# First attention layer: one full-width block of value matmuls between the two pairs of the next key tile; the rows of ones written at the end of the former batch

## The reference

```python
tokens = x.reshape(B, C, N).transpose(0, 2, 1)
qkv = (tokens @ w_proj + b_proj).reshape(B, N, NUM_HEADS, 3 * HEAD_DIM)
q, k, v = jnp.split(qkv, 3, axis=-1)
attn = jnp.einsum('bihd,bjhd->bijh', q, k) * SCALE
attn = jax.nn.softmax(attn, axis=2)
res = jnp.einsum('bijh,bjhd->bihd', attn, v).reshape(B, N, NUM_HEADS * HEAD_DIM)
out = res @ w_out + b_out + tokens
```

## Time and profile before

| | us |
|---|---|
| median of 3 runs | 3213.33 |
| lowest, highest | 3209.35, 3216.2 |
| span of the profiled execution, first to last instruction | 3214.9 |
| TensorE busy / VectorE / ScalarE / GpSimd | 2731.7 / 2212.3 / 1234.2 / 657.1 |
| matmuls | 16502 |
| mean granted TensorE clock (1 is 2.4 GHz) | 0.924 |

### The profile page before, as it was taken

The page is one execution under the profiler, slowest core; times in us unless marked ns, Lnnn a source line. Parts: engine busy times, 40 slices in busy tenths (PEclk is TensorE's granted clock), DMA queues, the critical chain, the costliest instruction groups (busy, mean ns, idle before and its releaser), DMA issues.

```text
span 3214.9 us, 45307 instructions
## 1 busy us (share of the span) xinstructions
PE 2731.7 (85%) x16502; PEld 1884.4 (59%) x16502; DVE 2212.3 (69%) x2474; ACT 1234.2 (38%) x1348; POOL 657.1 (20%) x397
## 2 busy tenths in 40 slices
PE   5889969899798897988879888798887998878983
PEld 4447754577545774457744677447764477644772
DVE  4766668666686675866668666785677756777666
ACT  2443325433254332543335333353333533244333
POOL 0430115201061021500225002340024300243011
PEclk8989989999899998999989999899988999889996
DMA  6100050000500004000040000400022000310015
GB/s 152 23 24 1 1 120 6 24 1 14 113 1 24 1 14 113 1 24 1 14 112 1 24 1 32 95 1 24 1 64 62 24 1 1 92 35 24 1 53 235
DMA packets 46400, 124.77 MB, mean 39 GB/s; under 512 B 9792, under 2 KB 21312, under 8 KB 42560
## 3 DMA queue, kind: packets, MB, share of 16 engines
q1 hardware_dynamic: 46144, 121.41, 14.1%
HBM read 43.01 MB, written 23.86 MB: 21 GB/s over the span
## 4 chain that ended last, share of the span: by engine, by line
PE 65%; DVE 12%; issue 9%; SPq 4%; DMA 4%; ACT 4%; DVEq 0%; ACTq 0%
PE tile L1264 22%; PE pv L1264 10%; PE tile L1358 8%; PE pv L1374 6%; PE tile L1336 5%; DVE small L871 4%; PE tile L1518 4%; SPq L445 4%; PE tile L1395 3%; DMA stack<-ones 2%; PE tile L1540 2%; PE tile L1648 1%; PE tile L1567 1%; PE tile L1417 1%; DMA stack<-qk_r 1%
## 5 line engine op out<-in xcount | busy, mean ns | idle before, releaser
L871 DVE TENSOR_REDUCE small<-tile 128x1 f32<-128x1024 f32 x512 | 610.6, 1219 | 210.9 <-PE tile L1336 210.1
L660 ACT ACTIVATE p<-tile 128x1024 f32<-128x1024 f32 x512 | 520.9, 1023 | 568.9 <-PE tile L1358 564.5
L1358 PE MATMUL tile<-stack 112*128 112x512 f32 x1024 | 387.0, 462 | 129.5 <-DMA stack<-ones 87.8
L547 POOL TENSOR_TENSOR acc<-acc,p 128x1024 f32<-128x1024 f32 x160 | 397.6, 2505 | 176.9 <-DVE acc L903 175.0
L1264 PE MATMUL tile<-qk_r 128*128 128x512 f32 x1536 | 378.0, 395 | 0.0
L1336 PE MATMUL tile<-stack 96*128 96x512 f32 x1024 | 339.8, 424 | 34.9 <-DMA stack<-qk_r 31.0
L1358 PEld LDWEIGHTS tile<-stack 112*128 112x128 f32 x1024 | 162.9, 196 | 350.7 <-issue 227.5
L572 POOL TENSOR_TENSOR row_sum<-act 128x256 f32<-128x256 f32 x32 | 42.1, 1335 | 1488.9 <-DVE act L1099 1488.9
L1374 PE MATMUL pv<-p,v 128*32 128x256 f32 (+1 forms) x3584 | 321.2, 431 | 9.4 <-ACT p L660 7.6
L1264 PEld LDWEIGHTS tile<-qk_r 128*128 128x128 f32 x1536 | 287.1, 188 | 66.6 <-issue 7.7
L1104 DVE TENSOR_TENSOR pl<-p,ph 128x1024 fp32r<-128x1024 f32 x128 | 158.2, 1236 | 238.2 <-ACT p L745 238.2
(11 more groups left out here) (277 smaller groups left out, 4356.9 us busy)
## 6 DMA issues: line engine op xcount, KB each, us to landing
stack<-qk_r SPq DMA_DIRECT2D x192, 256.0 KB, 5.0
x_in<-in_x_dram SPq DMA_DIRECT2D x9, 1024.0 KB, 7.6
act<-in_x_dram SPq DMA_DIRECT2D x8, 1024.0 KB, 11.0
x_scratch<-act SPq DMA_DIRECT2D x7, 1024.0 KB, 3.9
z_scratch<-zbuf SPq DMA_DIRECT2D x7, 1024.0 KB, 5.1
stack<-ones SPq DMA_DIRECT2D x8, 512.0 KB, 10.1
w3f<-w3f_scratch SPq DMA_DIRECT2D x8, 512.0 KB, 3.3
fin_rest<-z_scratch SPq DMA_DIRECT2D x3, 1024.0 KB, 12.6
```

The source lines that it names most:

```text
L547: pe.tensor_tensor(total, first, p0[:, jt % DEPTH, pair, :], ALU.add).then_inc(pool_done, gps.one("add0", *u, jt, pair))
L660: sc.activation(p0[:, jt % DEPTH, pair, :], tile_wait(b, "st0", *u, jt, pair), ACT.Exp, scale=float(D) ** -0.5).then_inc(scalar_done, scal ...
L871: ve.tensor_reduce(maxima[:, h * NT + it:h * NT + it + 1], t[:], X, ALU.max).then_inc(vector_done, vector.one("max0", g, h, it))
L1358: ins = mm(o[:, halves[k]], stack[0:K0, 1, g, h, jt * P:(jt + 1) * P], stack[0:K0, 0, g, h, halves[half]], start=True, stop=True)
```

## The change

`pv0` is no longer cut. For key tiles 0 to 6, all 512 columns of the four heads are done in one block, placed after the first pair (and the first `s0`) of the next key tile; nothing stands behind the second pair. The rows of ones for the next batch are written by SP after TensorE's step `g` of the batch, between the stores of x and z; those of the first batch before the loop, once the vector engine has finished its setup. The last batch writes none for a next one. The number of DMAs stays the same.

```diff
             for pair in range(2):
                 s += [("st0", *u, jt, pair)]
                 s += [("s0", *rows_of(next_unit(*u), 2 * jt + pair))] if next_unit(*u) else []
-
-                s += [("pv0", *u, 0)] if (jt, pair) == (1, 0) else []
-            s += [("pv0", *u, jt - 1)] if jt > 1 else []
+                s += [("pv0", *u, jt - 1)] if jt and pair == 0 else []
...
+            def key_ones():
+
+                sp.dma_start(stack[IMAX:K0, 1].rearrange("p g h (a n) -> p (g h a) n", n=P).bitcast(F32),
+                             ones[0:NMAX, :].rearrange("p (a n) -> p a n", a=1)
+                             .broadcast_to((NMAX, NG * G * N // P, P))).then_inc(key_ones_in, 16)
+
+            sp.wait_ge(vector_done, vector.count)
+            key_ones()
...
-                sp.dma_start(stack[IMAX:K0, 1].rearrange("p g h (a n) -> p (g h a) n", n=P).bitcast(F32),
-                             ones[0:NMAX, :].rearrange("p (a n) -> p a n", a=1)
-                             .broadcast_to((NMAX, NG * G * N // P, P))).then_inc(key_ones_in, 16)
...
                 sp.dma_start(x3_dram[b], act[:]).then_inc(x3_stored, 16)
+                sp.wait_ge(tensor_done, tensor.at(b, "g"))
+                key_ones()
                 sp.wait_ge(scalar_done, scalar.at(b, "z_kept", CT - 1))
...
-                def pv0(g, half, jt, part):
-
-
-                    if part == 0:
-                        scalar_wait("exp0", g, half, jt, 1)
-                        if jt == 0 and g == 1:
-                            scalar_wait("pv0_out", 0, half)
-
-                    whole = jt in (0, NT - 1)
-                    first, n = (0, HALF) if whole else (part * HALF // 2, HALF // 2)
-                    for h in range(G) if part == 0 or not whole else ():
-                        i, o = (k * HALF + first for k in (h % 2, half))
-                        ins = mm(pv[D * h:D * h + D, o:o + n], v0[:, jt, g * P + D * h:g * P + D * h + D],
-                                 p0[:, jt % DEPTH, h // 2, i:i + n], start=jt == 0, stop=jt == NT - 1)
-                    if part == (0 if whole else 1):
-                        ins.then_inc(tensor_done, tensor.one("pv0", g, half, jt))
+                def pv0(g, half, jt):
+
+                    scalar_wait("exp0", g, half, jt, 1)
+                    if jt == 0 and g == 1:
+                        scalar_wait("pv0_out", 0, half)
+                    for h in range(G):
+                        ins = mm(pv[D * h:D * h + D, halves[half]], v0[:, jt, g * P + D * h:g * P + D * h + D],
+                                 p0[:, jt % DEPTH, h // 2, halves[h % 2]], start=jt == 0, stop=jt == NT - 1)
+                    ins.then_inc(tensor_done, tensor.one("pv0", g, half, jt))
...
-                            if jt:
-                                pv0(*u, jt - 1, pair)
+                            if jt and pair == 0:
+                                pv0(*u, jt - 1)
...
                     if following:
-                        pv0(*u, NT - 1, 0)
-                        pv0(*u, NT - 1, 1)
+                        pv0(*u, NT - 1)
                         m0(*following)
                         den0(*u)
                     else:
                         den0(*u)
-                        pv0(*u, NT - 1, 0)
-                        pv0(*u, NT - 1, 1)
+                        pv0(*u, NT - 1)
```

## The result

| | before | changed |
|---|---|---|
| median of five runs each, us | 3213.33 | 3172.01 |
| lowest, highest | 3207.17, 3219.5 | 3170.8, 3190.89 |
| span of the profiled execution | 3214.9 | 3189.1 |
| ratio of changed to before | | 0.9877, 95% interval 0.985 to 0.9905 |

The change makes the kernel 1.2% faster. 3177 had been forecast. The profiled execution of the changed kernel is the slowest of its five, 3190.9; the other four lie between 3170.8 and 3172.2.

The account below looks back on a forecast made before the run. TensorE, busy 85% of the span, was the engine to follow, its longest wait being for the rows of ones. Terms -60, +26 and -2 sum to -36 us, from 3213.3 to 3177, range 3150 to 3203.

Parts of the forecast that it names:

- Part 1: Start of each batch's units: with the ones written earlier, TensorE's wait for them goes, -7.5 us a batch, -60 in all.
- The wait for the copies: Start of unit 0: ScalarE's first exponential, waiting for all 24 copies, is late next, starting at about 475.7 instead of 483.58.
- the median of the copies, 5.0 us: Start of unit 0: the last copy, issued at 470.60, was taken to land 5.0 us later, at 475.6.
- Part 2: First three units of a batch: scores wait for the exponential, key tile 3.51 us against 3.43, +1.1 a unit, +26 in all.
- 5.5 us in both orders, 0: Units 0 to 2, VectorE's stretch from S(4,1) to ST(6,0): claimed to be 5.5 us in both orders, effect 0.
- Part 3: Last unit of each batch: -0.3 us a batch, -2 in all, between -9 and +8.
- where the clock falls: Last unit: the clock falls behind the wait for VectorE today, and where it falls decides a us.
- my term for the work: Last unit: key tile 2.84 us against 2.46, 1.5 later but absorbed by the wait for VectorE; -0.3 a batch taken.
- Rival B: Last unit: new 0.6 us gaps lower the clock there, +2.3 to 2.7 a batch, 3197 us; chance 0.09.
- Rivals A: Units 0 to 2: no wait for the exponential, -3 instead of +26, 3148 us; chance 0.16.
- C: Units 0 to 2: gaps put key tiles at the low clock, 1.7 us more each, 3299 with nine; chance 0.05.
- D: Start of units: copies land late, at 480 rather than 475.6, gaining only 3 us a batch, 3213; chance 0.07.

Follow-up runs that it names:

- e1_ones: The kernel before with only the earlier writing of the ones, value blocks still in halves: 3147.9 us, ratio 0.9785.
- e6_late_copies: Ones early, whole blocks in the last unit only, plus ScalarE waiting for the 24 copies in steps instead of all at once: 3119.26 us, ratio 0.9696.
- e4_whole_short_exp: The changed kernel with exponentials over 512 of 1024 columns from key tile 4 of unit 0 on: 3156.99 us, ratio 0.9806.
- e2_whole: The changed kernel with the ones back behind the copies, so whole blocks alone: 3224.46 us, ratio 1.0025 against the kernel before.
- e7_short_pool: The changed kernel with GpSimd's additions of key tiles 2 and up over 512 of 1024 columns: 3146.5 us, ratio 0.9778.
- e8_late_copies_halves: `e6_late_copies` with half blocks in the last unit too: 3146.86 us, ratio 0.9782.
- e9_ones_shifted: `e1_ones` with six matmuls more in the first projection of each batch, output unchanged: 3147.79 us, ratio 0.9792.
- e5_halves_short_exp: `e1_ones` with exponentials over 512 of 1024 columns from key tile 4 of unit 0 on: 3147.69 us, ratio 0.9777.
- e10_late_copies_shifted: `e6_late_copies` with six matmuls more in the first projection of each batch, output unchanged: 3120.02 us, ratio 0.9712.

## Why the prediction held, point by point

**Part 1** was right in size and in mechanism. Forecast -7.5 a batch, -60; measured -7.44 (`e1_ones` to unit 1), -60. The wait for the copies was next, as said, and `e6_late_copies` took it away. The ones don't move the z store: in `e1_ones` it follows the x store by 30.4 to 30.5 us, as before, and lands in 4.8 to 5.6; the same ones are in the changed kernel, so they alone don't make the 34.2 of its profiled execution. The ones land in 7.6 us at their new place. One term was met by chance. The forecast took the median of the copies, 5.0 us, for the last one, which is what ScalarE waits for. Before, that one takes 6.48 to 6.75, with the ones issued behind it; with the ones gone from there it takes 4.60 to 4.82.

**Part 2** had the right period, 3.50 for the forecast 3.51, and the right cause: S waits for its slot in 96 places, 23.2 us, and where `e4_whole_short_exp` takes that wait away the period is 3.08. The sum of it was too high. +1.1 a unit was forecast; +0.40 (against `e1_ones`) or +0.59 (`e2_whole` against before) came in unit 0, +0.61 in units 1 and 2. Sum 1.62 a batch, 13 us for the 26. The term that failed is "5.5 us in both orders, 0" for VectorE's stretch: from S(4,1) to ST(6,0) it went from 504.85 - 499.34 = 5.51 to 495.30 - 490.38 = 4.92. A stretch that I read as VectorE's own work holds a wait for GpSimd's chain of four additions, which takes 9.52 us in both kernels. As TensorE runs 0.6 later against that chain, it finds 0.6 less to wait. 1.1 - 0.6 = 0.5 is close to the 0.61. `e7_short_pool` shows the coupling, with 4.22 for the same stretch; that just this offset is the 0.6 rests on the rows of the two kernels.

**Part 3.** Forecast -0.3 a batch for the last unit, with up to a us for where the clock falls. Measured -0.97. By work and waits the whole blocks are worse there, +0.36 (31.20 to 31.56); but the clock, which fell in five of eight batches before (32.65 to 34.29), stays up in all eight, and that is -1.33. The sign of my term for the work was wrong, the clock was inside the bound of -9. Rival B had the clock fall more because of the gaps; it falls less. In the six kernels with whole blocks there and full exponentials it fell in none of 48 batches. With halves it fell in 5 (before), 0 (`e1_ones`), 7 (`e8_late_copies_halves`) and 1 (`e9_ones_shifted`) of 8. Whole blocks alone don't keep it up: with short exponentials it fell in all 8 batches with them (`e4_whole_short_exp`) as with halves (`e5_halves_short_exp`).

**Not in the forecast** was the stretch behind the layer. It is 1.08 us a batch longer in the changed kernel than in `e1_ones` (184.71 and 183.63), and 1.10 shorter in `e6_late_copies`. This and the 1.98 of the layer (162.21 and 160.23) are the 24 us by which the change does worse than its one half: 8 x 3.06. TensorE idles at the second layer's start in all of them, the granted clock falls to 0.5 (1.2 GHz) there, and it rises again sooner or later. The stretch to the x store goes with that moment: 182.5 us where it rises 16.8 us behind the load's issue (`e6_late_copies`), 183.3 and 184.0 at 17.6 and 18.6 (two batches of `e1_ones`), 184.7 at 19.7 (changed).

**The sum.** -60 + 13 - 8 = -55 in the layer, 54 in the table; +7 or 8 behind it: -47. The medians differ by 41, and the interval of the ratio reaches from 31 to 48. Some 2 us of the rest is setup ahead of batch 0 (52.0 against 50.3; it lies between 51.0 and 53.0 in all experiments, with the ones early or late, so I don't put it down to the change); what is left lies inside that interval. So the forecast's -36 came within 5 us partly by luck, by errors of opposite sign: 13 us too much in part 2 and 6 too little in part 3, against 8 us not seen. Rivals A (a period of 3.2), C (units at the low clock; the granted clock is 1.00 from 480 on, 10 us into unit 0 of batch 1) and D (late copies; first exponential 8.3 sooner) are out.

**What stays open:** what decides whether the clock falls in the last unit, and when it rises behind it. The runs show that it does, and what it costs, and not more. `e9_ones_shifted` and `e10_late_copies_shifted` were to tell whether the moment of a gap decides it, and hardly moved the gaps. The same question stands behind the 34.2 and 30.5 us of one stretch in one execution of the changed kernel.

The best kernel is `e6_late_copies`: halves in units 0 to 2, whole blocks in the last, ones early, copies waited for in three steps. 3119.26 us, 3.0% under the kernel before, where the change as it was made gives 1.2%.

## What to carry to other kernels

Take a change with two halves apart: here the ones alone gave 2.15% and the whole change 1.2%, and only the one-part runs showed it. Fewer matmuls don't pay where the order they need makes scores wait for a buffer slot, and taking that wait away only brings up the next engine. And a stretch that "an engine sets" is to be looked at for a second engine inside it: compare one instruction's duration there with the shortest of its kind.

## What the runs showed of the hardware

- VectorE's additions with two inputs in SBUF and GpSimd's don't run beside each other: 1.22 us alone, 2.51 when begun 1.42 before GpSimd's end. VectorE's maxima, which read a score tile in PSUM, keep their 1.22 to 1.23 during GpSimd's chain. Halving GpSimd's additions cut the mean of VectorE's from 1595 to 1291 ns.
- Less work can cost time through the clock: in the last unit 31.20 us at full clock, 32.65 or 34.3 where it falls, in the same kernel.
- The copy of ones, 512 KB, lands in 10.1 us (median) behind 24 other copies and in 7.6 alone.
- At the loop's turn VectorE stands 3.9 to 4.5 us; of 1.36 us more of TensorE's work no more than 0.4 was left behind it.
